# Moving the write-back of dequantized weights from GpSimd's queue to SyncE's, inside an attention loop

## What is computed

```python
xn  = layernorm(x)
q,k = rope(xn @ Wq), rope(xn @ Wk);  v = xn @ Wv          # 16 heads of 64
s   = concat(softmax(causal(q k^T / 8)) v) @ Wo
h   = layernorm(xn) * gamma + beta
w1  = (fc1_q - 128) * fc1_scales   # int32 [1024, 4096], one scale row per 128 rows
w2  = (fc2_q - 128) * fc2_scales   # int32 [4096, 1024], one scale row per 128 rows
f   = xn + 0.5 * (silu(h @ w1 + b1) @ w2 + b2)
out = x + s * silu(f)
```

## The kernel before

| groups | K | jobs in the groups |
|---|---|---|
| 3, 6 | 4 | 1 each, of w1 |
| 9, 12 | 8 | 1 each, of w1 |
| 13, 14, 15, 16, 17 | 8, 8, 8, 12, 12 | 2, 2, 3, 2, 3, of w1 |
| 18 to 23 | 12 | 2, 3, 2, 3, 2, 2, of w2 |
| 24 to 30 | 16 | 3, 2, 3, 2, 3, 2, 3, of w2 |

## Time and profile before

### The profile page before, as it was taken

How to read it: one execution, slowest core, us unless ns; L and a number is a source line. 1 busy time by engine, 2 the same in 40 slices (tenths; PEclk the granted TensorE clock), 3 DMA queues, 4 the chain that set the end, 5 groups by cost and what they waited for, 6 DMA issues and landing times. The chain is left out here.

```text
span 1931.1 us, 16239 instructions; the slowest of 8 cores (1901.2 to 1931.1 us)
## 1 busy us (share of the span) xinstructions
PE 1180.7 (61%) x5186; PEld 424.8 (22%) x5250; DVE 680.9 (35%) x680; ACT 524.1 (27%) x593; POOL 346.5 (18%) x584
## 2 busy tenths in 40 slices
PE   0016856446354674233645566685699999699995
PEld 0013322112110110000111111111244444244442
DVE  1233554454457655333424434344111012300123
ACT  1231011101032453122524455563122210033100
POOL 0003311221253331111221221212100012000120
PEclk9999987767755666565666676776899999899998
DMA  4654122322142313545332332320854432322123
GB/s 142 153 173 125 66 66 59 72 44 44 44 87 68 92 50 121 161 163 166 96 125 84 107 122 97 127 92 33 272 167 149 147 120 99 114 71 77 61 98 109
DMA packets 83922, 205.72 MB, mean 107 GB/s; under 512 B 16496, under 2 KB 33152, under 8 KB 78464
## 3 DMA queue, kind: packets, MB, share of 16 engines
q1 hardware_dynamic: 66096, 147.51, 25.3%
q10 hardware_dynamic: 8864, 29.38, 5.0%
q0 software_dynamic: 8880, 27.79, 4.6%
HBM read 163.21 MB, written 37.76 MB: 104 GB/s over the span
## 5 line engine op out<-in xcount | busy, mean ns | idle before, releaser
L779 ACT ACTIVATE ptb<-pbig,negub 128x1024 bf16<-128x1024 f32 x320 | 337.1, 1120 | 457.1 <-PE pbig L760 456.3
L809 PE MATMUL p<-ptb,v_tm 128*64 128x512 bf16 x640 | 172.0, 530 | 316.1 <-POOL ptb L789 258.7
L830 DVE RECIPROCAL lrec<-p 1x512 f32<-1x512 f32 x64 | 213.9, 3343 | 13.5 <-PE p L817 12.5
L760 PE MATMUL pbig<-q_att,k_att 64*128 64x512 bf16 x640 | 156.3, 503 | 35.4 <-ACT ptb L779 34.5
L817 PE MATMUL p<-ptb,ones_bf 128*1 128x512 bf16 x640 | 157.8, 489 | 0.0
L714 DVE SCALAR_TENSOR_TENSOR dq_o<-dq_i,dq_s 128x1024 bf16<-128x1024 int32 (+1 forms) x48 | 75.9, 1581 | 205.9 <-DMA w2deq<-dq_o 124.3
L809 PEld LDWEIGHTS p<-ptb,v_tm 128*64 128x64 bf16 x640 | 41.1, 118 | 427.2 <-issue 427.2
L948 PE MATMUL p<-h_fm,w1t 128*128 128x512 bf16 x497 | 117.3, 385 | 25.0 <-DMA w1t<-w1deq 12.3
L1127 DVE TENSOR_SCALAR t_f<-xb,negmu_a,r_a 128x1024 f32<-128x1024 f32 x16 | 13.0, 813 | 318.3 <-PE p L1106 179.1
L1072 PE MATMUL p<-h_fm,w1t 128*128 128x512 bf16 x502 | 112.4, 384 | 15.8 <-ACT y_sl L1080 15.1
L791 POOL TENSOR_TENSOR ptb<-ptb,msk_bf 128x128 bf16<-128x128 bf16 x256 | 108.7, 431 | 71.6 <-ACT ptb L779 71.2
(11 more groups left out here) (138 smaller groups left out, 1632.7 us busy)
## 6 DMA issues: line engine op xcount, KB each, us to landing
xb<-x SPq DMA_DIRECT2D x48, 512.0 KB, 4.4
w1t<-w1deq SPq DMA_DIRECT2D x96, 256.0 KB, 3.0
dq_i<-fc_q SPq DMA_DIRECT2D x16, 1024.0 KB, 6.6
dq_s<-fc_scales SPq DMA_DIRECT2D x16, 1024.0 KB, 10.7
dq_i<-fc_q SPq DMA_DIRECT2D x32, 512.0 KB, 4.1
dq_s<-fc_scales SPq DMA_DIRECT2D x32, 512.0 KB, 5.0
w1deq<-dq_o POOLq DMA_DIRECT2D x16, 512.0 KB, 10.7
w2deq<-dq_o POOLq DMA_DIRECT2D x32, 256.0 KB, 5.6
```

The source lines that it names most:

```text
L760: dst=(sc0 if jj == 0 else sc1): e.matmul(dst, k_att[r:r + 64, S * m + 128 * kt:S * m + 128 * (kt + 1)], q_att[r:r + 64, S * m + 512 * qg: ...
L779: sch.op("scalar", lambda e, pt=pt, half=half: e.activation(pt[:, 0:1024], pbig[:, 1024 * half:1024 * half + 1024], AF.Exp, bias=negub[:, ...
L809: K=K, gp=gp: e.matmul(obank[gp][cpos:cpos + 64, :], v_tm[:, 1024 * kt + 64 * h:1024 * kt + 64 * (h + 1)], pt[:, 512 * (cpos // 64):512 * ...
L830: sch.op("vector", lambda e, jj=jj, gp=gp: e.reciprocal(lrec[32 * jj:32 * jj + 1, :], bass.AP(lbank[gp], 32 * jj * 512, [[512, 1], [1, 512 ...
```

## The change

The write L719 is issued by SyncE instead of GpSimd, and it counts on a semaphore of its own, `dW3`, instead of on `dG0` and `dG1` by turns. VectorE's wait for the write of the job before, and the waits at the end of attention, follow.

```diff
                     if ji >= 1:
-                        sch.wait("vector", f"dG{(ji - 1) % 2}", dq_dg[ji - 1])
+                        sch.wait("vector", "dW3", dq_dg[ji - 1])
...
-                    sch.wait("gpsimd", "cVE", dq_ve[ji])
-                    sch.op("gpsimd", lambda e, dsth=dsth, cols=cols, bi=bi: e.dma_start(
-                        out=dsth, in_=dq_o[bi][:, 0:cols]), inc=f"dG{ji % 2}", k=16)
-                    dq_dg[ji] = sch.snap(f"dG{ji % 2}")
+                    sch.wait("sync", "cVE", dq_ve[ji])
+                    sch.op("sync", lambda e, dsth=dsth, cols=cols, bi=bi: e.dma_start(
+                        out=dsth, in_=dq_o[bi][:, 0:cols]), inc="dW3", k=16)
+                    dq_dg[ji] = sch.snap("dW3")
...
                     sch.wait(eng, "dG0")
                     sch.wait(eng, "dG1")
+                    sch.wait(eng, "dW3")
```

## The result

| what | us |
|---|---|
| median before, beside it (lowest, highest) | 1936.29 (1919.84, 1986.95) |
| median after (lowest, highest) | 1770.93 (1759.72, 1824.48) |
| ratio after to before, 95% interval | 0.9152 [0.9099, 0.9204] |
| attention (first to last reciprocal), 8 cores, before | 780.5 to 792.2 (core 6: 792.2) |
| the same, after | 612.2 to 623.8 (core 6: 618.3) |

The kernel is 8.5% faster. Attention explains all of it: a core in the middle of the eight went from about 782 to about 617 us, 165 us, and 8.5% of the 1925 us that most executions of the kernel before take is 164.

A forecast was written before the change was run, and what follows sets the result against it. Attention was taken as bound by one chain of VectorE's jobs, GpSimd's waiting write issues and masks, and TensorE's last tiles. 175 us saved less 5 gave 1762.6 from the profiled 1932.6; plus 17, 1780 us, range 1740 to 1845.

The forecast's parts named there:

- The mechanism: Attention groups: with the waiting issues off GpSimd's list, a period becomes the longer of two times instead of their sum.
- the bare pace: Period of an attention group without jobs: 14.4 us at K = 8, 21.4 at K = 16, about 18 at K = 12.
- The sum: Attention groups 3 to 30 with jobs: 175 us saved over their periods, 170 after a price of 5.
- W for w1: VectorE's wait between two w1 jobs of a group, for write and loads: stays 11.6 us, cannot go under 11.2.
- W for w2: VectorE's wait between two w2 jobs of a group, for write and loads: stays 6.5 us, cannot go under 5.5.
- Masks and L714: GpSimd's masks and VectorE's L714 in attention now meet and hold each other off: 5 us lost, upper end 22.
- The bare pace at K = 16: Attention groups 24 to 30: a group without jobs takes 21.4 us, taken for the three groups of two jobs.
- Slow issue: Rival, chance 0.12: SyncE issues 256-byte pieces slowly, 5.2 us ahead of w1's loads; 118 us saved, about 1831 us.
- Slower: Rival, chance 0.03: the write's landing grows with its pieces, 37 us for 2048; 85 us lost, about 2035 us.
- Series: Rival, chance 0.05: write and loads wholly one after the other, waits 21.9 and 11.1 us; 1929 us.
- More gain: Rival, chance 0.10: write lands first, loads set the waits, 11.2 and 5.9 us; 182 us saved, 1768 us.
- The level: Whole kernel: 17 us added to the profiled execution's 1932.6 us, so that no change would be 1949.6 us.

The follow-up runs named there:

- Experiment 1: Changed kernel, write still on SyncE, but GpSimd again waits for each L714 at the old place and issues nothing: 1897.94 us, ratio to the kernel before 0.9811.
- Experiment 2: Changed kernel with the write and its wait for L714 issued by ScalarE instead of SyncE: 2080.43 us, ratio to the kernel before 1.0719.
- Experiment 6: Changed kernel with jobs spread evenly, two output buffers and writes issued by GpSimd behind the group's last mask: 1711.62 us, ratio to the kernel before 0.8883.
- Experiment 8: Changed kernel with each group's first job ahead of the reciprocals: ratio to the kernel before 0.9029; with even spread 0.8807; with spread and buffers 0.8777.
- experiment 3: Changed kernel with SyncE issuing the next job's two loads ahead of the write, all behind the same L714: 1769.75 us, ratio to the kernel before 0.9198.

## Why the prediction was right

**The mechanism** was right. The waiting issue in GpSimd's list held the masks, TensorE and, through L842, VectorE itself; taken out, a group's period is the longer of VectorE's list and the bare pace. Experiments 1, 2 and 6 show this from three sides: the wait alone costs 6.6 of the 8.5%, a worse list is slower than before, and a harmless place in the old list costs nothing that can be told.

**The sum** was right to a microsecond by luck. The stretches of the table took 673.9 us before and 499.1 after on core 6, 174.8 saved, where the gross sum said 175 (170 with the price of 5). All of attention on core 6 lost 173.9. But its terms missed on both sides: groups 13 to 17 came out 6.1 us under the forecast, and groups 9, 12 and 18 to 30 together 6.4 over it. Core 6 was also some 10 us slower there before than the typical core, most of it in groups 13 to 17 (200.5 against a median of 194.2). The typical core saved 165 us, 5 less than the net forecast.

**W for w1 was sized too high**: 11.6 was taken, 10.1 measured, under the 10.5 to 12.5 that were named as a sign, and 11.2 was called a bound that it could not go under. The failing step was to read the scale load's landing of 10.7 us, from one core, as a bound of the loads alone. Five other cores of the same execution have 8.9 to 9.1 us there, beside the same write by GpSimd, and the cores of after 8.2 to 9.2. So most of the difference is core 6's in that execution, and only some tenths are the change's: the median W of w1 went from 10.6 to 10.1 us. Why three cores of before had 10.4 to 10.7 stays open. On core 6, seven waits of 1.5 us are 10 us. Of these 3.3 came back as something that the sum did not have: the first job of a group waits, too, for its scales (0.90, 1.57 and 0.78 us), when the jobs before have just used the one buffer. In group 14 on core 6:

```profile
744.56 2.29 DVE L714 SCALAR_TENSOR_TENSOR dq_o<-dq_i,dq_s 128x2048 bf16<-128x2048 int32 x1 [0.90 <-DMA dq_s<-fc_scales]
```

**W for w2** was taken at 6.5 and came out at 6.1 on core 6. Its floor, 5.5, held. By the Trainium skill ("DMA: Bandwidth & Descriptors", section "Issuing engines are not separate DMA queues") another issuer saves its issue time only, and W would have stayed at 11.6 and 6.5. For w2 the trace of core 6 is within 0.4 us of that; for w1 it differs by 1.5, the median core by 0.5. The landing of the write itself differs by far more, 3.9 against 10.7.

**Masks and L714** were priced at 5 us, on VectorE's list. Groups of core 6 over the attention part of after (line, engine, operation, shapes, count, busy us, mean ns, idle before):

```profile
L791 POOL TENSOR_TENSOR ptb<-ptb,msk_bf 128x128 bf16<-128x128 bf16 x256 | 131.1, 518 | 425.3 <-ACT ptb L779 425.3
...
L714 DVE SCALAR_TENSOR_TENSOR dq_o<-dq_i,dq_s 128x1024 bf16<-128x1024 int32 x32 | 40.0, 1249 | 116.3 <-DMA dq_s<-fc_scales 115.9
L714 DVE SCALAR_TENSOR_TENSOR dq_o<-dq_i,dq_s 128x2048 bf16<-128x2048 int32 x16 | 37.0, 2313 | 74.2 <-DMA dq_s<-fc_scales 74.0
```

And the same of before:

```profile
L791 POOL TENSOR_TENSOR ptb<-ptb,msk_bf 128x128 bf16<-128x128 bf16 x256 | 108.7, 431 | 71.6 <-ACT ptb L779 71.2
...
L714 DVE SCALAR_TENSOR_TENSOR dq_o<-dq_i,dq_s 128x2048 bf16<-128x2048 int32 x16 | 36.7, 2293 | 81.3 <-DMA w1deq<-dq_o 81.0
```

L714 grew by 20 to 24 ns each (from 2293 and, for w2, 1225 ns), 1.1 us over 48. The masks paid: 22.4 us more over 256. Where it shows on the path is in groups 9 and 12, whose jobs stand beside the masks of a short group. How much of the rest lies on the path was not measured. On core 6 in group 9 (with line and engine as above):

```profile
658.51 2.41 DVE L714 SCALAR_TENSOR_TENSOR dq_o<-dq_i,dq_s 128x2048 bf16<-128x2048 int32 x1
...
658.87 2.33 POOL L791 TENSOR_TENSOR ptb<-ptb,msk_bf 128x128 bf16<-128x128 bf16 x1
...
661.35 0.41 PE L809 MATMUL p<-ptb,v_tm 128*64 128x512 bf16 x2 [2.95 <-POOL ptb L791]
```

A mask that takes 0.43 us alone took 2.33, until L714 was over, and TensorE waited 2.95 us for it. The two groups took 31.2 us where the bare pace is 28.8, and this wait is larger than the difference of 2.4; on the median core they took 32.7. Experiment 8 takes the loss away by moving the job off the masks. The Trainium skill ("SBUF — State Buffer", section "SBUF: two separate sides") calls the port pair an exclusive lock that is held for a whole instruction; this row agrees. The term was charged to the wrong engine: 5 us were taken, for delayed L714; these were 1.1, and the held masks of groups 9 and 12 cost 2.4 on core 6 and 3.9 on the median core.

**The bare pace at K = 16** was read from one group. The three groups of two jobs there (25, 27, 29) took 22.8 to 23.3 us instead of 21.4, 4.8 us more together; the four of three jobs took 24.0 to 28.1, 1.6 less together than four times 25.9. What made the former longer stays open.

**The rivals.** *Slow issue* fell: SyncE issues a w1 write of 2048 pieces in 0.38 us and a w2 write in 0.33. *Slower* fell with it: 2048 pieces land in 3.9 us, not 37. *Series* fell as well: W is not above what it was. *More gain* gave the mechanism of W, a write that is long landed while the loads set the end, but as a ratio its time is 1768 / 1949.6 = 0.907, outside the interval. By the rule of the Trainium skill beside it ("DMA: Bandwidth & Descriptors", section "Queues, rings and completion order") a write ahead in the loads' ring goes first; experiment 3 agrees, 10.1 against 3.9 us. In W it was nearer than the forecast, which took no change: on the median core W fell by 0.5 us for w1 and 0.3 for w2, where this rival said 0.4 and 0.6. Its 12 us more did not come as time.

**The level** of the forecast, 17 us above the profiled execution, rested on two executions; with more, the kernel before stands at 1936.29 instead of 1949.6, and 1936.29 x 0.9152 = 1772. As a ratio the forecast was 1780 / 1949.6 = 0.913.

## What to carry to other kernels

A DMA issue that waits for another engine's result is an instruction in its engine's list, and everything behind it waits, too. Before asking which queue is faster, look at what stands behind the issue on its engine; an idle engine, or a place behind the work that others wait for, takes the wait away at no cost that could be told here. Then the next limit shows: here the serial list of reciprocals, jobs and their load waits on VectorE, which an even spread of the jobs and one job ahead of the reciprocals shortened by another 4%.

## What the runs showed of the hardware that was not expected

- The same 512 KB write in 256-byte pieces lands (medians of core 6) in 3.9 us at the head of SyncE's queue, in 10.1 behind 2 MB of loads in that queue, in 9.9 from ScalarE's queue and in 9.7 to 10.7 from GpSimd's, beside the loads. The wait between two jobs changed far less: 10.6 us on the median core before, 10.1 after, 11.2 with the loads ahead.
- When masks on GpSimd and L714 on VectorE meet, GpSimd loses nearly everything: 22.4 us more over 256 masks (87 ns on a mean mask of 431), against 1.1 us over 48 L714.
- One core's median landing can mislead: in one execution the scale load of w1 landed in 8.9 us on some cores and in 10.7 on another.
- TensorE's clock rose with the denser work. The windows of core 6 from its first reciprocal to that of group 31 (start:end us, length, busy us of PE, PEld, DVE, ACT, POOL with counts, granted clock, DMA share, GB/s), of after:

```profile
562.13:1177.08 614.95, 417.12 (x1958) 101.42 (x1954) 352.11 (x234) 332.82 (x316) 170.61 (x434) 0.71 0.45 136
```

And of before:

```profile
554.72:1343.48 788.76, 439.64 (x1958) 101.50 (x1954) 349.92 (x234) 332.89 (x316) 183.77 (x482) 0.64 0.34 107
```

The same work took TensorE 22.5 us less, at a mean granted clock of 0.71 of 2.4 GHz instead of 0.64. Both are mixtures of the two levels. Two windows in and behind group 26 of after show one each:

```profile
1041.00:1055.00 14.00, 11.79 (x70) 3.46 (x68) 4.63 (x5) 11.38 (x11) 4.81 (x13) 0.97 0.48 125
1056.00:1064.00 8.00, 5.82 (x22) 1.04 (x20) 5.53 (x4) 3.92 (x4) 0.00 (x0) 0.50 0.61 220
```

0.97 is in effect 2.4 GHz and 0.50 is 1.2 GHz. Between them TensorE had waited four times for masks, 0.55 to 1.09 us each; a pair of L809 takes 0.41 us in the first and 0.64 in the second. How much of the 165 us is due to this was not tried apart; in TensorE's own time it is at most the 22.5.
